# One more early table, a merged gram unit and a reordered chunk 2 in a DLRM interaction tower

## The chip, the cores and the metric

One Trainium2 chip, one core. The metric is the device time of one execution in microseconds (us), as the median of several runs. Its engines are named as the profile does: PE (TensorE, matmuls and transposes), DVE (VectorE), ACT (ScalarE), POOL (GpSimd, which issues the indirect gathers) and SP (SyncE, which issues the plain DMAs).

## What is computed

512 samples have 27 categorical features each. Every feature has a table of rows of 128 floats (1,000 to 125,000 rows). For each sample the 27 rows are looked up, all dot products of two different rows are taken, and a small dense network follows:

```python
e = jnp.stack([tbl_0[ids[:, 0]], ..., tbl_26[ids[:, 26]]], axis=1)   # 512 x 27 x 128
interactions = jnp.einsum('bfd,bgd->bfg', e, e)                      # 27 x 27 per sample
x = interactions.reshape(B, F * F)[:, TRIL_IDX]                      # 351 pairs
z = jnp.concatenate([bottom_mlp_out, x], axis=1)
h = jnp.concatenate([z, r_bottom_mlp_out], axis=1)                   # 607
h = jnp.maximum(h @ W_top1 + b_top1, 0.0)                            # 512
h = jnp.maximum(h @ W_top2 + b_top2, 0.0)                            # 256
y = h @ W_top3                                                       # 512 x 1
```

## The kernel before, in words

The samples are worked on in four chunks of 128. What a chunk needs is its transposed embeddings `ET` (128 values on the partitions, then sample and feature). They come in two ways.

Features whose table has 1,000 rows can be looked up without a gather. `plan_tables` (L49) picks `N_ONE_HOT` = 9 of the twelve such tables as early ones, which serve all four chunks, and `N_LATE` = 2 late ones, which serve chunks 2 and 3. SP loads each whole table (0.5 MB, two DMAs, L273 and L274) and the feature's ids as int16, broadcast to all partitions (L269), into a ring of `TABLE_RING` = 5 buffers. ACT casts the table to fp32r (`high`, `make_high`, L352), DVE subtracts to get the remainder (`low`, L462, four parts). The one-hot matrix `hot` of 8 blocks of 125 rows by 512 samples is made by DVE (L465, 7 or 6 blocks) and ACT (L363 and L368, 1 or 2 blocks). PE multiplies (`look_up`, L551): 8 blocks with `high` and 8 with `low`, in the order high 0 to 3, low 0 to 3, high 4 to 7, low 4 to 7, 512 columns each (256 for a late table). ACT moves the sum into `ET` (`move_lookup`, L371). `hot`, `high` and `low` are double buffered, so table n is prepared only when table n-2 is looked up. Ahead of the first table PE runs `sum(WARM_UP)` = 34 matmuls on zeros (L545).

All other features are gathered: POOL issues one indirect DMA per feature and chunk (L309), 128 rows of 512 bytes, chunk after chunk: 18 each for chunks 0 and 1, 16 each for chunks 2 and 3, 68 in all. Neighbouring features form a run of up to four; `runs` (L113) lists them, and the last run of chunk 3 is split in two. PE transposes a run into one of two PSUM banks (`transpose_run`, L523), and DVE (even runs) or ACT (odd runs) moves it to `ET` (`move_run`, L317). A run waits on PE for its rows and for the mover of the run two before it (`free_pt`, L515).

A chunk's pair products are grams (`gram_unit`, L602, L613): for 32 groups of four samples a small matmul per sample, in units of 16 groups for chunks 0 to 2 and of 8 for chunk 3 (`sizes`, L106). When a unit is done, DVE and ACT copy half of it each into `Z` (`move_gram`, L325, eight copies per engine). When all units of a chunk are copied, SP packs the rows with five small DMAs (`pack`, L244, and `pack_extra`, L250); for chunk 3 SP, ACT and POOL share them. Then come layer 1 (`dense_layer1_bottom`, L591, and three calls of `pair_tile`, L618, here called the pairs), relu on ACT (`relu_h1`, L395), layer 2 on PE (`dense_layer2`, L530) and layer 3 on DVE (`dense3`, L473, bias add, then product and sum).

Every engine has its order written out by hand, and each runs its instructions strictly in that order. On PE, chunk c's loop (L631) does the first gram unit of c, `BETWEEN[c]` runs of c+1, the pairs of c-1, the second unit of c, more runs, layer 2 of c-1, the rest of the runs. The pairs of chunk 2 stand inside chunk 3's grams (L678, `AFTER_DENSE1`, between the second and the third unit), layer 2 of chunk 2 behind them:

```python
            for k in units_of(LAST):
                if k == AFTER_DENSE1:
                    wait_packed(LAST - 1)
                    for t in range(TILES):
                        done = pair_tile(LAST - 1, t)
                    done.then_inc(dense1, 1)
                gram_unit(k)
            dense_layer2(LAST - 1)
```

The functions that the change touches, and what calls them:

## Time and profile before

| | us |
|---|---|
| median of the runs | 121.84 |
| lowest and highest of the 3 runs | 120.61, 122.99 |
| the profiled execution, its own time | 119.64 |
| its span, first to last instruction | 117.5 |

| engine | busy, us | share of the span |
|---|---|---|
| PE | 92.8 | 79% |
| DVE | 74.8 | 64% |
| ACT | 63.7 | 54% |
| POOL | 72.8 | 62% |

How to read it: the span is that of one profiled execution, and every time in a row is counted from its start. Busy time leaves out waiting; it says how much an engine had to do, not whether the end waited for it. An entry such as `[1.84 <-DMA rows<-in_tbl,ids_sb]` in a timeline says that the engine was idle for 1.84 us before the instruction and what ended that time. The matmuls of grams and layers appear as two records each in the trace; lookups, transposes and warm-ups as one. Start and length of rows overlap by a little, since matmuls and copies are pipelined; rates are therefore taken from start to start.

### The profile page before, as it was taken

The numbers are of one execution on the slowest core, as the hardware profiler recorded it, in microseconds if no ns is written. First come the engines' busy times: TensorE is split into PE (matmuls) and PEld (weight loads), VectorE is DVE, ScalarE is ACT, GpSimd is POOL, SyncE is SP. The second block draws the span as 40 slices with busy tenths as digits, with TensorE's granted clock in tenths as the row PEclk, the third lists the DMA queues.
The fourth block names the chain that finished last, engine by engine and source line by source line (L and its number), as shares of the span: only waits on it lengthen the run. The fifth ranks groups of instructions, "written<-read, shape, count | busy, mean of one in ns | idle before, by whom it ended". The sixth has DMA issues, their size and how long they took to land.

```text
span 117.5 us, 3583 instructions
## 1 busy us (share of the span) xinstructions
PE 92.8 (79%) x1464; PEld 77.8 (66%) x1464; DVE 74.8 (64%) x230; ACT 63.7 (54%) x150; POOL 72.8 (62%) x75
## 2 busy tenths in 40 slices
PE   6608999999899999794458399955899838992992
PEld 6503788878688788583357299843798718980990
DVE  5418899999999999864994062164154656793001
ACT  7525698997996985563162162361165506990010
POOL 2777777777777787777777777677677620001000
PEclk9999999999999999999999967999999999999689
DMA  3749999999999767793112212113122220000000
GB/s 39 164 132 261 252 248 237 242 244 247 230 242 234 179 165 214 290 300 92 46 45 76 62 50 67 50 50 86 49 59 59 58 58 6 0 6 21 0 0 1
DMA packets 7347, 14.28 MB, mean 121 GB/s; under 512 B 2149, under 2 KB 4485, under 8 KB 7332
## 3 DMA queue, kind: packets, MB, share of 16 engines
q1 hardware_dynamic: 5104, 9.58, 32.8%
q0 software_dynamic: 2208, 4.47, 14.5%
q8 instruction: 11, 0.18, 0.6%
q14 instruction: 4, 0.03, 0.1%
q10 hardware_dynamic: 20, 0.01, 0.1%
HBM read 13.81 MB, written 0.00 MB: 118 GB/s over the span
## 4 chain that ended last, share of the span: by engine, by line
POOL 59%; issue 18%; PE 10%; DMA 6%; DVE 3%; ACTq 1%; DVEq 0%
POOL rows L309 59%; PE pH L587 5%; DMA rows<-in_tbl,ids_sb 3%; DVE Z L342 3%; PE pT L587 2%; PE pG L613 2%; DMA ids_sb<-in_ids 2%; DMA Z<-Z 1%; PE pF L538 1%; ACTq L247 1%; PE pT L527 1%; DVE prod L484 0%; DVE ET L321 0%; DVEq L129 0%
## 5 line engine op out<-in xcount | busy, mean ns | idle before, releaser
L309 POOL DMA_INDIRECT rows<-in_tbl,ids_sb x68 | 71.6, 1054 | 21.6 <-issue 20.4
L465 DVE TENSOR_SCALAR hot<-ids_b,row_f 125x512 fp32r<-125x512 int16 (+1 forms) x75 | 31.8, 452 | 1.7 <-DMA ids_b<-in_ids_t 1.7
L342 DVE COPY Z<-pG 26x96 f32<-26x96 f32 (+1 forms) x80 | 19.5, 244 | 19.5 <-PE pG L613 18.5
L342 ACT COPY Z<-pG 26x96 f32<-26x96 f32 (+1 forms) x80 | 18.7, 234 | 16.3 <-PE pG L613 15.4
L563 PE MATMUL pG<-hot,high 125*128 125x512 f32 x72 | 22.0, 422 | 4.7 <-ACT high L352 4.2
L563 PE MATMUL pG<-hot,low 125*128 125x512 f32 x72 | 20.2, 404 | 0.0
L462 DVE TENSOR_TENSOR low<-tbl,high 125x256 fp32r<-125x256 f32 x44 | 18.2, 414 | 3.1 <-ACT high L352 3.1
L563 PEld LDWEIGHTS pG<-hot,high 125*128 125x128 f32 x72 | 13.6, 196 | 9.3 <-ACT high L352 4.5
L613 PE MATMUL pG<-ET 128*26 128x26 f32 x1024 | 13.5, 194 | 7.1 <-issue 4.6
L613 PEld LDWEIGHTS pG<-ET 128*26 128x26 f32 x1024 | 11.2, 104 | 10.1 <-issue 7.9
L563 PEld LDWEIGHTS pG<-hot,low 125*128 125x128 f32 x72 | 14.1, 196 | 3.1
L352 ACT CAST high<-tbl 125x1024 fp32r<-125x1024 f32 x11 | 11.5, 1048 | 8.2 <-DMA tbl<-in_tbl 5.9
L527 PE MATMUL pT<-ident,rows 128*128 128x128 f32 x68 | 11.4, 291 | 5.6 <-DMA rows<-in_tbl,ids_sb 1.8
L587 PE MATMUL pH<-Z,W1Z 128*128 128x128 f32 x84 | 12.2, 311 | 1.9 <-DMA Z<-Z 1.9
L527 PEld LDWEIGHTS pT<-ident,rows 128*128 128x128 f32 x68 | 8.1, 145 | 7.9 <-issue 3.0
L587 PEld LDWEIGHTS pH<-Z,W1Z 128*128 128x128 f32 x84 | 11.7, 225 | 2.3 <-DMA Z<-Z 2.2
L321 DVE COPY ET<-pT 128x256 f32<-128x256 f32 (+2 forms) x13 | 6.4, 494 | 6.7 <-PE pT L527 6.6
L321 ACT COPY ET<-pT 128x512 f32<-128x512 f32 (+3 forms) x12 | 5.8, 488 | 8.3 <-PE pT L527 8.2
L363 ACT ACTIVATE away<-ids_b,row_f 125x512 f32<-125x512 int16 x13 | 9.4, 722 | 0.1
L368 ACT ACTIVATE hot<-away 125x512 fp32r<-125x512 f32 x13 | 8.2, 633 | 0.4
L538 PE MATMUL pF<-W2S,H1T 128*128 128x256 f32 x32 | 7.7, 383 | 0.0
L247 POOL DMA_DIRECT2D Z<-Z x1 | 0.6, 555 | 11.5 <-DVE Z L342 11.5
(39 smaller groups left out, 57.6 us busy)
## 6 DMA issues: line engine op xcount, KB each, us to landing
tbl<-in_tbl SPq DMA_DIRECT2D x11, 448.0 KB
ids_b<-in_ids_t SPq DMA_DIRECT2D x9, 128.0 KB, 5.2
rows<-in_tbl,ids_sb POOLq DMA_INDIRECT x68, 5.0
W1Z<-in_w_tiles SPq DMA_DIRECT2D x1, 768.0 KB
tbl<-in_tbl SPq DMA_DIRECT2D x11, 52.0 KB
W1A_B<-in_w_ab SPq DMA_DIRECT2D x1, 512.0 KB, 3.8
W2S<-in_W_top SPq DMA_DIRECT2D x1, 512.0 KB
botT<-in_bottom_t SPq DMA_DIRECT2D x1, 256.0 KB, 4.0
```

Source lines behind the costliest of these rows:

```text
L309: pool.indirect_dma_start(out=rows[:, c % 2, slot[f], :], out_offset=None, in_=tables[f][:, :], in_offset=bass.IndirectOffsetOnAxis(ap=ids ...
L321: engine_copy(ET[:, c, :, f0:f0 + n, :].rearrange("d q f a -> d f q a"), pT[pt_order.index((c, i)) % 2][:, 0:n * P].rearrange("d (f q a) - ...
L342: last = engine_copy(to[:, :, STAGE - n:STAGE, :, s, :], of)
L352: nc.scalar.copy(high[0:TP, n % 2, :, :], tbl[0:TP, n % TABLE_RING, :, :]).then_inc(high_done, 1)
L363: nc.scalar.activation(away[0:TP, :], ids_b[0:TP, n % TABLE_RING, :], ACT.Abs, scale=-1.0, bias=row_f[0:TP, k:k + 1]).then_inc(away_done, 1)
L462: nc.vector.tensor_tensor(low[0:TP, n % 2, at, :], tbl[0:TP, n % TABLE_RING, at, :], high[0:TP, n % 2, at, :], ALU.subtract).then_inc(low_ ...
L465: nc.vector.tensor_scalar(hot[0:TP, n % 2, k, columns(n)], ids_b[0:TP, n % TABLE_RING, columns(n)], row_f[0:TP, k:k + 1], None, ALU.is_equ ...
L527: last = nc.tensor.transpose(bank[:, x * P:(x + 1) * P], rows[:, c % 2, slot[f], :], ident[:, :])
L538: last = nc.tensor.matmul(pF[:, :], H1T[:, k, :], W2S[:, k, :], start=k == 0 and c < LAST, stop=k == K1 - 1)
L563: last = nc.tensor.matmul(lookup_bank(n), part[0:TP, n % 2, k, :], hot[0:TP, n % 2, k, columns(n)], start=x == 0 and k == 0, stop=x == 3 a ...
L587: done = nc.tensor.matmul(bank[:, at * P:(at + 1) * P], weights[:, k * P:(k + 1) * P], acts, start=first and clears, stop=last, skip_group ...
L613: last = nc.tensor.matmul(pG[QUAD * s:QUAD * s + GRAM_ROWS, at:at + TOGETHER * COLS], some.rearrange("d s f -> d (s f)")[:, 0:GRAM_ROWS], ...
```

## The change

- `N_ONE_HOT` is 10: feature 14 becomes an early table, features 17 and 25 are the late ones. Gathers per chunk are 17, 17, 15 and 15, 64 in all. Chunks 2 and 3 have one run more than before (7 and 8).
- Warm-up is 72 matmuls. Table 0 is loaded and cast in two halves of four blocks (`pieces`), with a semaphore of its own for the first half.
- SP no longer waits for the first ids before it asks for table 1, nor for the last table or `W1A_B` before it asks for the weights.
- DVE makes all one-hot blocks of a table first and then the four `low` parts; `look_up` runs high 0 to 7, then low 0 to 7. ACT moves the lookup of table n-1 ahead of the one-hot blocks of table n+1.
- Grams of chunks 0 to 2 are one unit of 32 groups each. Chunk 3 keeps four units of 8, with nothing between them.
- `prepare` and `look_up` of the late tables, layer 1 and 2 of each chunk, and relu and layer 3 get new places. Layer 1, relu, layer 2 and layer 3 of chunk 2 all stand inside chunk 2's loop, ahead of the last runs of chunk 3. The wait for the weights moves from the first loop to `dense_layer2`.
- `packed` is one semaphore per chunk.

The diff, cut to its core (names of the new lines are those of the changed kernel):

```diff
-N_ONE_HOT = 9
+N_ONE_HOT = 10
...
-WARM_UP = (20, 14)
+WARM_UP = 72
...
-    sizes = [[16, 16]] * LAST + [[8, 8, 8, 8]]
+    sizes = [[32]] * LAST + [[8, 8, 8, 8]]
...
+        def pieces(n):
+
+            return 1 + (n == 0)
...
                 elif n >= IN_FLIGHT:
                     sp.wait_ge(tbl_in[n - IN_FLIGHT], 32)
-                elif n:
-                    sp.wait_ge(ids_b_in[n - 1], 16)
...
-            sp.wait_ge(tbl_in[N_ALL - 1], 32)
             sp.dma_start(W1A_B[:, :, :], w1_ab).then_inc(w1ab_in, 16)
...
-            sp.wait_ge(w1ab_in, 16)
...
                 if n + 1 < N_ONE_HOT:
                     make_high(n + 1)
-                    one_hot_blocks(n + 1)
                 if n:
                     move_lookup(n - 1)
+                if n + 1 < N_ONE_HOT:
+                    one_hot_blocks(n + 1)
...
                 for k in range(TABLE_K - act_blocks[n]):
-                    part = k - 1
-                    if 0 <= part < LOW_PARTS:
...
                     nc.vector.tensor_scalar(hot[0:TP, n % 2, k, columns(n)], ids_b[0:TP, n % TABLE_RING, columns(n)],
                                             row_f[0:TP, k:k + 1], None, ALU.is_equal).then_inc(hot_done, 1)
+                for at in (slice(k, k + step) for k in range(0, TABLE_K, step)):
+                    dve.wait_ge(high_done, n + 1 + (n > 0 or at.stop > TABLE_K // 2))
+                    nc.vector.tensor_tensor(low[0:TP, n % 2, at, :], tbl[0:TP, n % TABLE_RING, at, :],
+                                            high[0:TP, n % 2, at, :], ALU.subtract).then_inc(low_done, 1)
...
+                runs_of(c + 1, 2, 4)
                 if c:
                     dense3(c - 1)
-                runs_of(c + 1, RUNS[c + 1] - LATE_RUNS[c + 1], RUNS[c + 1])
+                if c + 1 == LAST:
+                    dense3(c)
+                runs_of(c + 1, 4, RUNS[c + 1])
...
+                for k in units_of(c):
+                    gram_unit(k)
+                next_run()
+                next_run()
                 if c == 0:
                     look_up(N_ONE_HOT)
+                    next_run()
+                    look_up(N_ONE_HOT + 1)
+                    next_run()
+                    dense_layer1_bottom(c)
                 else:
+                    dense_layer1_pairs(c - 1)
+                    next_run()
+                    dense_layer2(c - 1)
+                if c + 1 < LAST:
+                    while len(waiting):
+                        next_run()
+                    if c:
+                        dense_layer1_bottom(c)
+                else:
+                    dense_layer1_bottom(c)
+                    dense_layer1_pairs(c)
+                    next_run()
+                    dense_layer2(c)
+                    while len(waiting):
+                        next_run()
...
             for k in units_of(LAST):
-                if k == AFTER_DENSE1:
-                    wait_packed(LAST - 1)
-                    for t in range(TILES):
-                        done = pair_tile(LAST - 1, t)
-                    done.then_inc(dense1, 1)
                 gram_unit(k)
-            dense_layer2(LAST - 1)
```

Where instructions stand now. First PE at the start of the program (`warm` is the warm-up operand, `hot`, `high` and `low` those of the lookup, x the count of equal instructions in a row). Before:

```order
L545 MATMUL pF<-warm 128x128 x34
L563 MATMUL pG<-hot,high 128x512 x4
L563 MATMUL pG<-hot,low 128x512 x4
L563 MATMUL pG<-hot,high 128x512 x4
L563 MATMUL pG<-hot,low 128x512 x4
```

And in the changed kernel:

```order
L541 MATMUL pF<-warm 128x128 x72
L557 MATMUL pG<-hot,high 128x512 x8
L557 MATMUL pG<-hot,low 128x512 x8
L557 MATMUL pG<-hot,high 128x512 x8
L557 MATMUL pG<-hot,low 128x512 x8
L522 MATMUL pT<-ident,rows 128x128 x2
```

The warm-up is more than twice as long, and a table's lookup is one group of eight with `high` and one with `low`.

Second, PE from chunk 2's grams to chunk 3's (`pG<-ET` are grams, `pT<-ident,rows` transposes of gathered rows, `pH<-botT,W1AB` the bottom part of layer 1, `pH<-Z,W1Z` the pairs, `pF<-W2S,H1T` layer 2). Before:

```order
L613 MATMUL pG<-ET 26x26 x64
L587 MATMUL pH<-botT,W1AB 128x128 x4
L587 MATMUL pH<-Z,W1Z 128x128 x12
L613 MATMUL pG<-ET 26x26 x64
L527 MATMUL pT<-ident,rows 128x128 x6
L538 MATMUL pF<-W2S,H1T 128x256 x4
L587 MATMUL pH<-botT,W1AB 128x128 x4
L527 MATMUL pT<-ident,rows 128x128 x10
L613 MATMUL pG<-ET 26x26 x64
L587 MATMUL pH<-Z,W1Z 128x128 x12
L613 MATMUL pG<-ET 26x26 x64
L538 MATMUL pF<-W2S,H1T 128x256 x4
```

And in the changed kernel:

```order
L607 MATMUL pG<-ET 26x26 x128
L522 MATMUL pT<-ident,rows 128x128 x6
L581 MATMUL pH<-Z,W1Z 128x128 x12
L522 MATMUL pT<-ident,rows 128x128 x2
L534 MATMUL pF<-W2S,H1T 128x256 x4
L581 MATMUL pH<-botT,W1AB 128x128 x4
L581 MATMUL pH<-Z,W1Z 128x128 x12
L522 MATMUL pT<-ident,rows 128x128
L534 MATMUL pF<-W2S,H1T 128x256 x4
L522 MATMUL pT<-ident,rows 128x128 x6
L607 MATMUL pG<-ET 26x26 x128
```

The pairs of chunk 1 moved behind the first two runs of chunk 3, and the pairs and layer 2 of chunk 2 moved from inside and behind chunk 3's grams to before its last transposes.

Third, DVE at the same place (`Z<-pG` are copies of grams, `ET<-pT` moves of transposed runs, `H<-pF,b_sb` and `prod,y<-H,W3S` the two instructions of layer 3). Before:

```order
L342 COPY Z<-pG 26x2x3x8x2 x3
L342 COPY Z<-pG 26x10x8x2
L321 COPY ET<-pT 128x2x64x2 x2
L321 COPY ET<-pT 128x4x64x2
L481 TENSOR_TENSOR H<-pF,b_sb 128x256
L484 SCALAR_TENSOR_TENSOR prod,y<-H,W3S 128x256
L321 COPY ET<-pT 128x64x2
L342 COPY Z<-pG 26x2x3x4x2 x3
```

And in the changed kernel:

```order
L343 COPY Z<-pG 26x160x2
L322 COPY ET<-pT 128x2x64x2 x2
L477 TENSOR_TENSOR H<-pF,b_sb 128x256
L480 SCALAR_TENSOR_TENSOR prod,y<-H,W3S 128x256
L477 TENSOR_TENSOR H<-pF,b_sb 128x256
L480 SCALAR_TENSOR_TENSOR prod,y<-H,W3S 128x256
L322 COPY ET<-pT 128x64x2
L322 COPY ET<-pT 128x2x64x2
L343 COPY Z<-pG 26x2x3x4x2 x3
```

Layer 3 of chunk 2, which stood behind all copies of chunk 3, now stands ahead of the moves of chunk 3's runs 4 and 6.

## Rows read from the trace of the kernel before

**Rows 1.** The page, 40 equal slices: busy tenths of PE, granted clock.

```profile
PE   6608999999899999794458399955899838992992
...
PEclk9999999999999999999999967999999999999689
```

**Rows 2.** The page: chain that ended last, by engine; the gathers' group.

```profile
POOL 59%; issue 18%; PE 10%; DMA 6%; DVE 3%; ACTq 1%; DVEq 0%
...
L309 POOL DMA_INDIRECT rows<-in_tbl,ids_sb x68 | 71.6, 1054 | 21.6 <-issue 20.4
```

**Rows 3.** Windows of L309: stretch, its length, busy (count), PEclk, DMA share, GB/s.

```profile
9.35:48.88 39.53, 31.61 (x26) 1.00 0.96 237
48.88:93.92 45.04, 34.06 (x37) 0.96 0.27 77
```

**Rows 4.** Timeline of POOL: start, length, what, idle before.

```profile
40.72 1.65 POOL L309 DMA_INDIRECT rows<-in_tbl,ids_sb  x1 [0.30 <-issue]
```

**Rows 5.** Timeline of all engines, from 92 us to the end.

```profile
92.08 3.06 SPq L247 DMA_DIRECT2D Z<-Z  x4
...
93.92 0.94 POOL L309 DMA_INDIRECT rows<-in_tbl,ids_sb  x1 [0.31 <-issue]
...
95.11 0.41 DVE L481 TENSOR_TENSOR H<-pF,b_sb 128x256 f32<-128x256 f32 x1
...
96.30 0.61 PE L527 MATMUL pT<-ident,rows 128*128 128x128 f32 x3 [1.84 <-DMA rows<-in_tbl,ids_sb]
...
97.34 1.32 PE L613 MATMUL pG<-ET 128*26 128x26 f32 x128 [0.43 <-DVE ET L321]
...
98.12 3.56 DVE L342 COPY Z<-pG 26x48 f32<-26x48 f32 x16 [0.88 <-PE pG L613]
...
102.26 3.56 DVE L342 COPY Z<-pG 26x48 f32<-26x48 f32 x16 [0.57 <-PE pG L613]
...
108.94 2.48 PE L587 MATMUL pH<-Z,W1Z 128*128 128x128 f32 x12 [1.85 <-DMA Z<-Z]
...
111.46 0.38 ACT L403 ACTIVATE H1T<-pH 128x256 f32<-128x256 f32 x1 [5.77 <-PE pH L587]
...
113.32 1.89 PE L538 MATMUL pF<-W2S,H1T 128*128 128x256 f32 x8
```

**Rows 6.** Timeline of PE, warm-up, table 0, and the first grams.

```profile
1.14 3.81 PE L545 MATMUL pF<-warm 128*128 128x128 f16 x34 [1.14 <-DVE warm L443]
9.16 3.12 PE L563 MATMUL pG<-hot,high 125*128 125x512 f32 x4 [4.21 <-ACT high L352]
12.07 1.90 PE L563 MATMUL pG<-hot,low 125*128 125x512 f32 x4
...
15.66 1.07 PE L563 MATMUL pG<-hot,high 125*128 125x512 f32 x4
...
48.84 1.81 PE L613 MATMUL pG<-ET 128*26 128x26 f32 x128 [0.73 <-issue]
```

**Rows 7.** Timelines of SP, DVE and ACT, 5 to 14 us.

```profile
6.25 0.43 SPq L273 DMA_DIRECT2D tbl<-in_tbl  x1
...
5.94 0.49 DVE L465 TENSOR_SCALAR hot<-ids_b,row_f 125x512 fp32r<-125x512 int16 x1 [1.66 <-DMA ids_b<-in_ids_t]
...
13.68 0.42 DVE L462 TENSOR_TENSOR low<-tbl,high 125x256 fp32r<-125x256 f32 x1 [0.34 <-ACT high L352]
...
8.06 1.04 ACT L352 CAST high<-tbl 125x1024 fp32r<-125x1024 f32 x1 [3.65 <-DMA tbl<-in_tbl]
...
12.61 1.04 ACT L352 CAST high<-tbl 125x1024 fp32r<-125x1024 f32 x1 [2.21 <-DMA tbl<-in_tbl]
```

**Rows 8.** Timelines of PE (two calls of the pairs) and DVE (copies of a unit of 16).

```profile
69.48 3.98 PE L587 MATMUL pH<-Z,W1Z 128*128 128x128 f32 x24
...
84.89 2.84 PE L587 MATMUL pH<-Z,W1Z 128*128 128x128 f32 x24
...
89.82 2.23 DVE L342 COPY Z<-pG 26x96 f32<-26x96 f32 x8 [2.98 <-PE pG L613]
```

More of the change, by code:

```diff
@@ L550, in look_up @@
                     pe.wait_ge(lookup_moved, n)
-                half = TABLE_K // 2
-                first, second = range(half), range(half, TABLE_K)
-                for x, (part, blocks) in enumerate(((high, first), (low, first), (high, second), (low, second))):
-                    if x == 0:
-                        pe.wait_ge(high_done, n + 1)
-                    for k in blocks:
+                for part in (high, low):
+                    for k in range(TABLE_K):
+                        if part is high and k % (TABLE_K // 2) == 0:
+                            pe.wait_ge(high_done, n + 1 + (n > 0 or k > 0))
                         if part is high and k < TABLE_K - act_blocks[n]:
@@ L564, in look_up @@
                                                 hot[0:TP, n % 2, k, columns(n)],
-                                                start=x == 0 and k == 0, stop=x == 3 and k == TABLE_K - 1)
+                                                start=part is high and k == 0, stop=part is low and k == TABLE_K - 1)
                 last.then_inc(looked_up, 1)
```

114 lines of the change are left out of this document (41 added, 73 removed).

## The prediction

> **What bounds the kernel now.** I read the page first, by slices, then the chain of waits, then the timelines of the stretches that the chain names. The slices show three stages: up to about 50 us (slice 17; a slice is 2.94 us) PE is at nine tenths; then it is half idle; its clock falls twice, in slices 23 and 24 and in 37 and 38 [rows 1]. The chain that ended last says what limits the middle: 59% of the span is POOL at the gathers of L309, and 18% "issue", mostly the pause between two of them, so POOL issues 68 gathers without one wait on another engine [rows 2]. The timeline of POOL gives the pace. 26 gathers issued from 9.35 to 48.88 us are 39.53 / 26 = 1.520 us apart, the 36 that start from 48.88 on are 45.04 / 36 = 1.251 us apart (the view counts 37, the one that starts at its end with them), with the DMA engines 96% busy at 237 GB/s in the first stretch and 27% in the second [rows 3]; the last starts at 93.92 [rows 5]. PE's wait for those rows ends at 96.30, 2.4 us later; grams of chunk 3 start at 97.34; 20.16 us from there to the end of the span (117.5) are a serial tail [rows 5]. So the time is: gathers until 93.92, 3.42 us to the grams, then the tail.
>
> The one-hot stage (9 to 48 us) isn't on that chain, but PE, DVE and ACT are all full in it, so a tenth table could put it there. The profiled execution took 119.64 us outside for a span of 117.5; the median of the runs shown is 121.84. I work in the span of the profile and add the difference to the median. Under about 2% (2.4 us) a change can hardly be told from none here.
>
> **The gathers.** Ten early tables instead of nine: features that are still gathered fall from 18, 18, 16, 16 per chunk to 17, 17, 15, 15, so 64 instead of 68. Four fewer at 1.251 us is 5.0 us off POOL's queue [rows 3]. Against it stands the slower pace during the one-hot stage: 26 x (1.520 - 1.251) = 7.0 us were lost there, with nine tables' work on DVE beside it. At 7.0 / 9 the tenth costs 0.8 us. Bounds: nothing (then the last gather starts at 88.9), and all 26 gathers at the worst row, 1.65 + 0.30 = 1.95 us apart, 11 us more [rows 4]; I take 0.8, as the total of DVE's work grows by a ninth and only its order changes. The last gather then starts at 93.92 - 5.0 + 0.8 = 89.7.
>
> The Trainium skill has a rule that speaks against this change: in "SBUF — State Buffer", section "SBUF: two separate sides", it says that while VectorE is in a two-port performance mode GpSimd is locked out and "cannot write the descriptors" of its DMAs. Taken whole, it would make VectorE's one-hot instructions, now six or seven in a row, a price on each gather beside them. By it the sum would be that of rival B below; by the row's 0.8 us it is the one here. The trace agrees in part (1.52 against 1.25 us), but the pace also goes with a full DMA, and no run here parts the two.
>
> **The one-hot stage.** One table is 16 matmuls of 512 columns; four take about 0.91 us from start to start, so 3.65 us, and with transposes and waits before, 8 tables from 15.66 to the end of the stage (48.84 less the 0.7 us of the last move) took 32.4 us, 4.05 each [rows 6]. The tenth table costs PE 4.05 us. What pays for it is the start. In before, PE warms until 4.95, then waits 4.21 us; its first four matmuls take 3.12 us, as each waits for a one-hot of DVE, which makes one at 5.94 and then stands behind the high part, started by ACT at 8.06; the next four take 1.90 us instead of 1.07, that is the clock's lower level, 1.2 GHz instead of 2.4; table 0 ends at 15.66 [rows 6, 7]. In after DVE makes all seven of table 0's one-hots from 5.94 on, before anything waits on it; the table arrives in two halves, and 72 warm-ups (34 x 0.112 = 3.8 us, then 38 at 0.056 to 0.112) keep PE busy until 7.1 to 9.2. Table 0 is then 3.65 us, ending near 12. Table 1 was cast from 12.61 on because it was asked for only at 6.25 [rows 7]; SP doesn't wait for the ids any more and asks at about 4. Its 0.63 MB (0.50 of table, 0.13 of ids) at 237 GB/s [rows 3] behind table 0 (8.1) is an estimate of 10.7 to 11, no later than 12.6 at worst. PE starts table 1 at about 12.0 instead of 15.66, and 9 x 4.05 = 36.5 brings the end to 48.5 instead of 48.1: the tenth table is free to within half a microsecond (from -1 to +2). DVE agrees: its lows of table 1 start at about 12.1 instead of 13.68 [rows 7], its one-hots of that table are already made, and from there it had no idle time in before. The order high x 8, low x 8 costs nothing: the lows are needed 1.8 us later than before. The gram unit of 32 in chunks 0 to 2 costs PE nothing (same 128 matmuls); on DVE and ACT 8 copies of double size replace 16. Eight copies of a unit of 8 take half of 3.56 us, 1.78 [rows 5]; of a unit of 16, 2.23 [rows 8]; 0.45 us for doubling 56 elements on the mean gives +0.9 for doubling 112, so 3.1 us instead of 4.46. Bounds: 2.23 and 4.46. They start one unit later, and the packing of chunk 2 rests on them, below.
>
> Would the rest of the stage hold up the middle? Chunk 1's grams follow about 13 us behind chunk 0's start (two late tables, their moves, the last runs): 62 instead of about 65. From there PE has 9 us of work (grams, runs, layer 1 and 2 of chunk 0), to 71. Chunk 2's last row is gather 49, issued at 89.7 - 15 x 1.251 = 70.9, landed near 73.9. So there are 3 us of cover: the early stage may be 3 us late and cost nothing.
>
> **Chunk 2 and the chain to the last grams.** This is where the order hurts. The rows for run 1 of chunk 3 end with gather 55, issued at 89.7 - 9 x 1.251 = 78.4. With a landing of 2.4 us [rows 5] to half as much again, 3.6 (an estimate; I take 3.0) PE may transpose at 81.4. Behind those transposes there now stand, in order on PE, both chunks' layers. Prices: layer-1 pairs 2.84 us for 24 records [rows 8], bottom a third of that (8 records, 0.95), layer 2 1.89 less the 0.15 in which its last record only ends, the relu's first half 0.38 [rows 5]. So: transposes to 81.9; pairs(1) to 84.75; relu 85.15; layer 2 (1) 86.9; bottom(2) 87.8; pairs(2) 90.7 (its packing: grams of chunk 2 from 75.2, 2.7 us, copies 3.1, five issues by SP 3.8, as four take 3.06 [rows 5], and under 2 to land, as copies end at 105.82 and PE starts at 108.94 in the tail with two issues between, 86.6, so hidden by 1.2 us); relu and hand-off 91.15; layer 2 (2) 93.1 with its latency. DVE has layer 3 of chunk 2 in front of the move of run 4 (0.41 us and about as much for its second half, 0.9 in all [rows 5]): 94.0; move 94.3. Run 6 shares run 4's bank, so it is transposed only now; from transposes to grams took 97.34 - 96.30 = 1.04 us [rows 5]: 95.3, and 0.3 us for some ten hand-offs: grams of chunk 3 at 95.6. The rows of gather 64 are there at 92.1 to 93.3. So 5.0 us taken off POOL move the grams by 97.34 - 95.6 = 1.7 us only; the rest goes into layer 1 and 2 of chunk 2, which now stand ahead of the last grams.
>
> **The tail.** Before: 0.78 us to the first copy, 16 copies, a wait of 0.57 for the third unit (PE had pairs(2) in between), 16 copies, end 105.82: 8.5 us. After: the four units' grams are in one piece, so 0.78 + 32 x 0.2225 = 7.9 us. From there on the chain is the same, 117.5 - 105.82 = 11.7 us [rows 5]. 95.6 + 7.9 + 11.7 = 115.2. The clock: pairs(3) ran 4.38 us from 108.94 to 113.32 instead of 2.84, and two slices show 6 and 8 tenths after PE had done 0.2 of a slice [rows 1, 5]. PE is now idle for some 7 us before it, so all of it may be at the lower level: up to 2 x 2.84 - 4.38 = 1.3 us more. It may also find the same phase. I take 0.4. Forecast span 115.6, 1.9 us less, on the median 121.84 - 1.9 = 119.9.
>
> **The rivals.**
> (A) The clock falls on the new chain. PE has only two transposes between chunk 2's grams (77.9) and 81.4. A gap like this stood before the pairs of chunk 0: 24 records took 3.98 us instead of 2.84 [rows 8], slices 6 and 7 [rows 1]. Price 1.1 to 1.9 us on the chain and up to 1.3 in the tail: 115.2 + 1.5 + 1.3 = 118.0 (median 122.3), just slower than before. Against: other thin stretches (slices 18, 19, 21) left it at 9. It decides when both falls come, over 2.3 us.
> (B) DVE's one-hots in a row hold POOL harder. The one gather of 1.65 us lay in such a stretch [rows 4]. If gathers beside them (60% of the stage) are issued every 1.95 us and others every 1.52, the mean is 1.78, 26 x 0.26 = 6.8 us more than my pace, everything behind POOL: 115.6 + 6.8 - about 1 that the lesser pace saves elsewhere, 121 to 122 (median 126). It beats the gain from 2 us of added issue time on. Against: DVE's total is the same, and another gather beside such a stretch is not slow.
> (C) The gain comes out whole: rows land in 2.4 us, the added 0.8 doesn't show, and pairs(3) finds the higher level: 115.2 - 0.8 - 0.6 - 1.5 = 112.3 (median 116.7).
> (D) The change doesn't do what it says: PE's own pauses ("issue" in the grams, hand-offs) fill the chain: 117.5 as before.
>
> **How the numbers follow.** Forecast 0.40 (114.6 to 116.5 in span, medians 118.9 to 120.8), A 0.20, B 0.08, C 0.18, D 0.14. Faster by over 2% means a median under 119.4: all of C and 0.16 of the forecast, 0.34, say 0.35. Slower by over 2%, over 124.3: B and 0.02 of A, 0.10. The rest 0.55. The range takes in C but for its far end and A: 117.5 to 122.6.
>
> **What would show it.** Right: 64 gathers, the last starting at 89 to 90.5; table 1's matmuls at about 12 and chunk 0's grams at 48 to 50; chunk 3's run 1 waiting for its rows until 81 to 82; pairs(1), pairs(2) and layer 2 back to back behind it; PE's last wait before the grams for DVE, not for rows; grams at 95 to 96.5; 32 copies without a gap; idle PE before pairs(3) some 7 us. Wrong: grams right behind the last rows (then the chain was shorter than I say), gathers of 1.5 us and more in the one-hot stage (B), PEclk at 5 around 82 to 86 (A), or chunk 2's grams later than 77, with PE never waiting for rows in chunk 2.

## The result and the profile after

The changed kernel took 132.75 us (median of four, 131.88 to 134.15); the kernel before took 121.22 us beside it (120.29 to 122.99). The ratio is 1.0955, 95% interval [1.0818, 1.1092]. Forecast were 119.9 us and a range of 117.5 to 122.6. A ratio here and below is formed from the executions within about 1.5% of the fastest of their kernel, a median from all of them, so a ratio can differ a little from the quotient of the medians. The profiled execution took 132.68 us for a span of 130.9, 13.4 us more than before.

Three places part those 13.4 us: the last gather starts at 103.09 instead of 93.92 (+9.2, forecast -4.2); from there to the grams of chunk 3 it is 6.50 instead of 3.42 us (+3.1); from the grams to the end 21.3 instead of 20.2 (+1.1).

The page of the kernel after (busy tenths of PE and POOL, granted clock; the gathers' group and the chain by engine), to be held against [rows 1, 2]:

```profile
PE   6978899999459499975759758848398875536792
...
POOL 2879888999978888987777877777778600001000
PEclk9999999999977999999999999999999999755579
...
POOL 51%; issue 16%; PE 15%; DVE 6%; DMA 6%; SPq 2%; ACTq 1%; ACT 0%; DVEq 0%
...
L310 POOL DMA_INDIRECT rows<-in_tbl,ids_sb x64 | 81.9, 1280 | 20.5 <-issue 18.6
```

There are 64 gathers, four fewer, but they keep POOL busy 81.9 us instead of 71.6: 1280 ns for one instead of 1054. PE has holes in slices 10, 11 and 13 (counted from 0), where in [rows 1] it was full until slice 17. The windows say in which stretch the gathers became slow:

```profile
9.00:55.60 46.60, 40.20 (x22) 0.96 0.86 221
55.60:103.09 47.49, 35.91 (x39) 1.00 0.22 58
```

From 55.6 us on it is 47.49 / 38 = 1.250 us from gather to gather, as in [rows 3] (39 are counted with the one that starts at the end). Before that, 22 gathers take 46.6 us: 2.12 us each, against 1.52. So the pace behind the one-hot stage is as before; the loss sits in that stage, beside a DMA that is less busy (0.86) than it was before (0.96). The timeline of POOL and DVE in that stage shows it in single instructions:

```profile
14.30 1.83 POOL L310 DMA_INDIRECT rows<-in_tbl,ids_sb  x1 [0.30 <-issue]
15.13 2.85 DVE L457 TENSOR_SCALAR hot<-ids_b,row_f 125x512 fp32r<-125x512 int16 x7
...
21.96 1.42 DVE L461 TENSOR_TENSOR low<-tbl,high 125x256 fp32r<-125x256 f32 x4
22.46 3.81 POOL L310 DMA_INDIRECT rows<-in_tbl,ids_sb  x1 [0.30 <-issue]
23.30 2.85 DVE L457 TENSOR_SCALAR hot<-ids_b,row_f 125x512 fp32r<-125x512 int16 x7
26.08 1.41 DVE L461 TENSOR_TENSOR low<-tbl,high 125x256 fp32r<-125x256 f32 x4
26.58 3.74 POOL L310 DMA_INDIRECT rows<-in_tbl,ids_sb  x1 [0.30 <-issue]
...
27.76 2.44 DVE L457 TENSOR_SCALAR hot<-ids_b,row_f 125x512 fp32r<-125x512 int16 x6
30.13 1.41 DVE L461 TENSOR_TENSOR low<-tbl,high 125x256 fp32r<-125x256 f32 x4
30.63 3.81 POOL L310 DMA_INDIRECT rows<-in_tbl,ids_sb  x1 [0.30 <-issue]
31.47 2.85 DVE L457 TENSOR_SCALAR hot<-ids_b,row_f 125x512 fp32r<-125x512 int16 x7
...
51.77 3.93 POOL L310 DMA_INDIRECT rows<-in_tbl,ids_sb  x1 [0.30 <-issue]
...
53.40 2.18 DVE L457 TENSOR_SCALAR hot<-ids_b,row_f 125x256 fp32r<-125x256 int16 x8
```

A gather that is under way when DVE begins its row of seven one-hots (23.30) ends at 26.27, 0.12 us behind the row (26.15). The next begins during the low parts, meets the next row and ends with it (30.32 and 30.20). Three times in a row the same, and again at 51.77 beside the eight short one-hots of a late table. It is not so with every row: of the eleven gathers under way when a row of six or more began, these four ended with the row; the seven others ended inside it, 0.2 to 1.0 us after its start, and took 0.94 to 2.62 us, as the one of 14.30, which ends at 16.13 while its row lasts until 17.98. The four alone are some 10.6 us over gathers of 1.16 us; the longer ones among the others make up the rest of the 13.4 us by which the last gather missed the forecast.

From the rows of chunk 3's run 1 to the last grams, PE of the kernel after, to be held against [rows 5] and the second order above:

```profile
94.42 0.66 PE L522 MATMUL pT<-ident,rows 128*128 128x128 f32 x4 [0.43 <-DMA rows<-in_tbl,ids_sb]
94.91 2.84 PE L581 MATMUL pH<-Z,W1Z 128*128 128x128 f32 x24
...
98.32 1.97 PE L534 MATMUL pF<-W2S,H1T 128*128 128x256 f32 x8 [0.27 <-ACT H1T L407]
100.12 1.05 PE L581 MATMUL pH<-botT,W1AB 128*128 128x128 f32 x8
101.91 2.95 PE L581 MATMUL pH<-Z,W1Z 128*128 128x128 f32 x24 [0.74 <-DMA Z<-Z]
...
105.42 1.97 PE L534 MATMUL pF<-W2S,H1T 128*128 128x256 f32 x8 [0.46 <-ACT H1T L407]
...
108.67 0.52 PE L522 MATMUL pT<-ident,rows 128*128 128x128 f32 x3 [0.96 <-DVE ET L322]
109.59 1.34 PE L607 MATMUL pG<-ET 128*26 128x26 f32 x128 [0.41 <-DVE ET L322]
112.84 1.70 PE L607 MATMUL pG<-ET 128*26 128x26 f32 x127 [1.92 <-DVE Z L343]
116.64 0.24 PE L607 MATMUL pG<-ET 128*26 128x26 f32 x1 [2.10 <-issue]
```

The two chunks' layers stand between the transposes at 94.42 and the grams at 109.59: 15.2 us in a row, of which only the last two waits are DVE's. The last line shows a third thing, that no term of the forecast had: one gram matmul waits 2.10 us for "issue", that is for nothing that the profile shows on another engine.

### The profile page after: what moved, and what is told of

It is laid out like the page before. It is cut to its first block, busy times and chain, and to the rows that moved or that the text cites. A ratio compares the mean times of both kernels' runs of the same rounds, so it can differ in the third digit from the quotient of the medians.

```text
span 130.9 us, 3675 instructions
## 1 busy us (share of the span) xinstructions
PE 99.7 (76%) x1514; PEld 83.6 (64%) x1514; DVE 75.2 (57%) x217; ACT 64.0 (49%) x134; POOL 83.0 (63%) x71
## 4 chain that ended last, share of the span: by engine, by line
POOL 51%; issue 16%; PE 15%; DVE 6%; DMA 6%; SPq 2%; ACTq 1%; ACT 0%; DVEq 0%
POOL rows L310 51%; PE pH L581 5%; DVE Z L343 5%; PE pG L607 5%; PE pF L534 3%; DMA Z<-Z 3%; SPq L249 2%; DMA rows<-in_tbl,ids_sb 2%; PE pT L581 2%; DMA ids_sb<-in_ids 1%; ACTq L249 1%; PE pT L522 1%; DVE prod L480 1%; DVE ET L322 0%; DVE H L477 0%
## 5 line engine op out<-in xcount | busy, mean ns | idle before, releaser
L310 POOL DMA_INDIRECT rows<-in_tbl,ids_sb x64 | 81.9, 1280 | 20.5 <-issue 18.6
L343 DVE COPY Z<-pG 26x48 f32<-26x48 f32 (+3 forms) x56 | 15.9, 284 | 17.8 <-PE pG L607 17.1
L343 ACT COPY Z<-pG 26x48 f32<-26x48 f32 (+3 forms) x56 | 15.0, 268 | 22.5 <-PE pG L607 21.8
L355 ACT CAST high<-tbl 125x1024 fp32r<-125x1024 f32 (+1 forms) x13 | 12.8, 983 | 13.8 <-PE pG L557 7.9
L557 PEld LDWEIGHTS pG<-hot,high 125*128 125x128 f32 x80 | 15.4, 201 | 6.4 <-ACT high L355 1.8
L322 DVE COPY ET<-pT 128x256 f32<-128x256 f32 (+3 forms) x14 | 6.3, 450 | 10.0 <-PE pT L522 9.9
L366 ACT ACTIVATE away<-ids_b,row_f 125x512 f32<-125x512 int16 x15 | 10.9, 724 | 0.2
L249 POOL DMA_DIRECT2D Z<-Z x1 | 0.6, 555 | 15.2 <-DVE Z L343 15.2
L371 ACT ACTIVATE hot<-away 125x512 fp32r<-125x512 f32 x15 | 9.5, 632 | 0.5
L322 ACT COPY ET<-pT 128x512 f32<-128x512 f32 (+2 forms) x13 | 5.7, 437 | 7.1 <-PE pT L522 7.0
L407 ACT ACTIVATE H1T<-pH 128x256 f32<-128x256 f32 x7 | 2.4, 385 | 13.0 <-PE pH L581 13.0
```

The lines of the kernel that those rows point to most:

```text
L310: pool.indirect_dma_start(out=rows[:, c % 2, slot[f], :], out_offset=None, in_=tables[f][:, :], in_offset=bass.IndirectOffsetOnAxis(ap=ids ...
L322: engine_copy(ET[:, c, :, f0:f0 + n, :].rearrange("d q f a -> d f q a"), pT[pt_order.index((c, i)) % 2][:, 0:n * P].rearrange("d (f q a) - ...
L343: last = engine_copy(to[:, :, STAGE - n:STAGE, :, s, :], of)
L355: nc.scalar.copy(high[0:TP, n % 2, ks, :], tbl[0:TP, n % TABLE_RING, ks, :]).then_inc(high_done, 1)
L366: nc.scalar.activation(away[0:TP, :], ids_b[0:TP, n % TABLE_RING, :], ACT.Abs, scale=-1.0, bias=row_f[0:TP, k:k + 1]).then_inc(away_done, 1)
L371: nc.scalar.activation(hot[0:TP, n % 2, k, :], away[0:TP, :], ACT.Relu, scale=-1.0, bias=1.0).then_inc(hot_act_done, 1)
```

## The experiments

Times of different runs are compared by their ratio to the kernel before on the same chip. On three chips the kernel before itself took 159 to 162 us. In the traces taken there, the kernels with ten tables have table transfers that stood still for 12 to 20 us; in the two with nine tables the transfers flow, and PE takes 39 and 38 us instead of 1.8 for the first gram unit, with pauses of 0.4 to 2.6 us between single matmuls. Of the runs there only the lengths of gathers and waits are used, not the times.

The theories. L (lock): a row of one-hots on DVE holds a gather that POOL has under way, up to the row's end; rows of six or seven cost the time, not DVE's total. F (fuller queue): the gathers are slow because SP asks for tables and weights earlier. C (chain): the layers of chunk 2 ahead of the last grams cost what they take, since PE and not the rows ends last there.

**1. The changed kernel with one-hots and low parts in turn.** Everything else stays, the earlier requests of SP too, so L and F part here.

```diff
                 for k in range(TABLE_K - act_blocks[n]):
+                    part = k - 1
+                    if 0 <= part < LOW_PARTS:
+                        ...
+                        nc.vector.tensor_tensor(low[...], tbl[...], high[...], ALU.subtract)
                     nc.vector.tensor_scalar(hot[...], ids_b[...], row_f[...], None, ALU.is_equal)
-                for at in (slice(k, k + step) for k in range(0, TABLE_K, step)):
-                    ...
```

> The changed kernel with DVE's order of before inside a table (one-hot, low, one-hot, low ... instead of seven one-hots and then four lows); all else stays. Theory L (one-hots in a row hold POOL's gather until the row ends): no gather over 2 us, the last of 64 starts at 89 to 91 us instead of 103.1, chunk 3's grams at 96 to 98, span 117 to 119 us, 12 to 14 us under the changed kernel. Theory F (the fuller DMA queue, asked for earlier and by one table more, slows the gathers): gathers of 3.8 us stay, the last starts after 100, span over 127. Theory C (the moved layers of chunk 2 and the tail cost most of it): span not under 127 either, though the gathers are faster.

> The changed kernel with DVE's order of before inside a table, run again, because the kernel before took 162 us beside it in the first go. Where the kernel before takes about 121 us: theory L (one-hots in a row hold POOL's gather until the row ends) expects the last gather at 89 to 91 us instead of 103.1, chunk 3's grams at 96 to 98, span 117 to 119 us. Theory F (fuller DMA queue) and theory C (moved layers and tail): span over 127.

> The changed kernel with DVE's order of before inside a table, third go, wanted beside a kernel before of about 121 us. Theory L (one-hots in a row hold POOL's gather until the row ends): last gather at 89 to 91 us instead of 103, chunk 3's grams at 96 to 98, span 117 to 120 us, ratio 0.97 to 1.00. Theory F (fuller DMA queue) and theory C (moved layers and tail): span over 127, ratio over 1.05.

The first two runs fell on chips of 160 us and more (170.86 against 162.03; 168.59 against 159.96): as times they say nothing of L. Their longest gathers were 2.05 and 1.56 us. The third was usable: 127.21 us (125.99 to 128.75) against 121.35, ratio 1.057 [1.041, 1.073]. DVE and POOL of this run:

```profile
26.79 0.48 DVE L464 TENSOR_SCALAR hot<-ids_b,row_f 125x512 fp32r<-125x512 int16 x1
27.19 0.42 DVE L461 TENSOR_TENSOR low<-tbl,high 125x256 fp32r<-125x256 f32 x1
27.27 1.16 POOL L310 DMA_INDIRECT rows<-in_tbl,ids_sb  x1 [0.30 <-issue]
...
28.65 0.42 DVE L461 TENSOR_TENSOR low<-tbl,high 125x256 fp32r<-125x256 f32 x1
28.73 1.65 POOL L310 DMA_INDIRECT rows<-in_tbl,ids_sb  x1 [0.30 <-issue]
28.99 1.27 DVE L464 TENSOR_SCALAR hot<-ids_b,row_f 125x512 fp32r<-125x512 int16 x3
```

A gather beside hot, low, hot takes 1.16 us; beside three one-hots in a row (28.99 to 30.26) it takes 1.65 us and ends with them, at 30.38. No gather of this run is longer. The last starts at 89.92; the forecast had 89.7. The order of DVE's instructions is what made the gathers slow: L stands, F falls. The runs show what the order does, and not by which shared part of the chip DVE holds POOL. But the grams of chunk 3 still start only at 105.25, 15.3 us behind the last gather: the 13 us that came back on POOL brought 4 on the end. I had expected 96 to 98 for these grams and a ratio of 0.97 to 1.00.

**2. The kernel before with one-hots in a row.** The converse: one edit in the kernel before, of DVE's order alone.

```diff
                 for k in range(TABLE_K - act_blocks[n]):
-                    part = k - 1
-                    if 0 <= part < LOW_PARTS:
-                        ...
                     nc.vector.tensor_scalar(hot[...], ids_b[...], row_f[...], None, ALU.is_equal)
+                for at in (slice(k, k + step) for k in range(0, TABLE_K, step)):
+                    ...
```

> The kernel before, and only DVE's order inside a table changed to that of the changed kernel (all one-hots, then four lows). Theory L: ten tables lost about 21 us of POOL's time in the changed kernel against 1.251 us per gather, so nine lose 19 instead of 7: the last gather starts at 105 to 107 instead of 93.9, span 129 to 131. Theory F and C: nothing in the DMA queues or in chunk 2 is changed, span 117 to 119.

> The kernel before with only DVE's order inside a table changed to one-hots in a row, run again for the same reason. Theory L: the last gather starts at 105 to 107 instead of 93.9, span 129 to 131. Theories F and C: 117 to 119.

> The kernel before with one edit: VectorE makes all one-hots of a table in a row and the four low parts behind them. Lock theory (a row of one-hots holds the gather that POOL has begun until the row ends): gathers of 2.5 to 4 us stand in the one-hot stage, the last gather starts 4 to 8 us later than 93.9, so at 98 to 102, and since the rows bound this kernel the end moves as far: span 122 to 126, ratio 1.04 to 1.07. If the lock needs the changed kernel's other edits (ten tables, the fuller queue): longest gather below 2.5 us, last gather within 1.5 us of 93.9, ratio within 1.02.

On chips of 160 us it took 165.07 (before 162.03) and 166.08 (before 159.96), with gathers of 4.61 and 3.51 us. On a usable one 127.56 us (125.29 to 131.06) against 123.08, ratio 1.026 [1.016, 1.036], less than I expected. Its profile (131.06 us, the longest execution of the six) has the row again:

```profile
40.78 3.52 POOL L309 DMA_INDIRECT rows<-in_tbl,ids_sb  x1 [0.31 <-issue]
41.31 2.87 DVE L458 TENSOR_SCALAR hot<-ids_b,row_f 125x512 fp32r<-125x512 int16 x7
44.08 1.44 DVE L462 TENSOR_TENSOR low<-tbl,high 125x256 fp32r<-125x256 f32 x4
44.60 3.14 POOL L309 DMA_INDIRECT rows<-in_tbl,ids_sb  x1 [0.30 <-issue]
45.42 2.20 DVE L458 TENSOR_SCALAR hot<-ids_b,row_f 125x256 fp32r<-125x256 int16 x8
```

40.78 + 3.52 = 44.30, the row's end is 44.18. The last gather starts at 103.66, 9.7 us later than before. So the row alone makes the kernel slower, with nine tables and the old requests. Here two of the gathers under way ended with the row of six or more, in the kernel after four; how many are held so long varies from run to run, and what decides it isn't shown.

**3. The changed kernel once more, as it is.**

> The changed kernel as it is, to have its trace and its ratio on the chips on which the kernel before took 160 to 162 us in the last two goes. All theories: if the chip is like those of the result, 131 to 134 us against 121. If it is like those of the last two goes, theory L expects gathers of 2 to 4 us where DVE makes one-hots in a row, and a ratio above the 1.075 of the interleaved kernel there; theory F and C the same ratio as that one, 1.06 to 1.09.

132.87 us (129.24 to 134.97) against 121.72; gathers of 3.81, 3.54 and 2.62 us and the last one at 101.40. The loss repeats, though only two of the gathers under way when a row began (3.81 and 3.54 us) ended with it; the rest of POOL's loss is in gathers of 1.7 to 2.6 us. The medians give 1.092; the shortest executions, 129.24 and 120.19 us, 1.075.

**4. The layers of chunk 2 late again**, in a kernel with one-hots in turn and in one with one-hots in a row. On PE (DVE and ACT follow):

```diff
                     dense_layer1_bottom(c)
-                    dense_layer1_pairs(c)
-                    next_run()
-                    dense_layer2(c)
...
             for k in units_of(LAST):
+                if k == UNITS_BY[LAST] - 2:
+                    dense_layer1_pairs(LAST - 1)
                 gram_unit(k)
+            dense_layer2(LAST - 1)
```

In turn:

> As the run before, and the pairs, relu, layer 2 and layer 3 of chunk 2 where the kernel before has them (inside and behind chunk 3's grams). If the chain of layers ahead of the last grams is what keeps the gain of fewer gathers away: chunk 3's grams start about 3.4 us after the last gather's start, as in before, at 93 to 94, and the tail is 20.2 us as before: span 113 to 115, 3 to 4 us less than the run before it. If that chain costs nothing: the same span as that run, 117 to 119.

> The same with the pairs, relu, layer 2 and layer 3 of chunk 2 where the kernel before has them, second go. If the chain of layers ahead of the last grams keeps the gain away: chunk 3's grams about 3.4 us after the last gather's start, at 93 to 94, span 113 to 115, ratio 0.95 to 0.97, 3 to 5 us under the run before it. If that chain costs nothing: the same span as that run.

In a row:

> The changed kernel with the layers of chunk 2 placed as before (pairs between the second and third gram unit of chunk 3, layer 2 behind the fourth, ReLU and layer 3 of chunk 2 as late), one-hots still in a row. With both theories (the lock sets the last gather, the early layers add to what follows it): last gather still at 101 to 103, grams of chunk 3 start 3.5 to 5 us behind it and not 6.5, tail 20 to 21, span 125 to 128, time 127 to 130 against 132.8. If the early layers were hidden under the wait for rows: the grams of chunk 3 start 6.5 us behind as before and the tail is longer by the moved layers, time 132 to 134. If they are worth the 7 us that they were with interleaved one-hots: 125 to 126.

The first went to a chip of 160 us (163.25 against 162.03). Usable: with one-hots in turn 120.07 us (119.15 to 122.44) against 121.35, ratio 1.000 [0.993, 1.007]; with one-hots in a row 128.50 (126.98 to 128.91) against 123.08, 1.047 [1.027, 1.067], last gather at 101.91 and grams of chunk 3 at 105.19, 3.3 us behind it. Four ratios make a table:

```
                     one-hots in a row   one-hots in turn
layers early              1.096               1.057
layers late               1.047               1.000
```

The row costs 3.9 and 4.7 points, the early layers 4.9 and 5.7: 5 to 6 us and 6 to 7 us of 121. Each ratio is known to 1 to 2 points, so the two add up as well as can be told (with the 1.075 above in the first corner the early layers would be 3 points there). L and C are both shown, and together they are the whole loss.

**5. Why nothing is gained without them.** In the last corner of the table the last gather starts at 89.72, 4.2 us before [rows 5], and the time is that of the kernel before. Page (chain) and timeline of PE of that kernel:

```profile
PE 68%; DVE 13%; issue 8%; DMA 5%; ACT 2%; SPq 1%; ACTq 1%; DVEq 0%
...
15.04 2.00 PE L559 MATMUL pG<-hot,high 125*128 125x512 f32 x8
...
52.18 3.47 PE L609 MATMUL pG<-ET 128*26 128x26 f32 x217 [0.73 <-issue]
...
86.15 0.66 PE L609 MATMUL pG<-ET 128*26 128x26 f32 x35 [2.23 <-issue]
86.74 1.54 PE L524 MATMUL pT<-ident,rows 128*128 128x128 f32 x6
88.08 3.50 PE L583 MATMUL pH<-Z,W1Z 128*128 128x128 f32 x24
...
97.22 1.32 PE L609 MATMUL pG<-ET 128*26 128x26 f32 x128 [0.40 <-ACT ET L322]
```

The chain that ended last is PE's at 68%, and POOL, 59% in [rows 2], isn't on it. Table 1 starts at 15.04; from there to the end of the stage (51.45) it is 36.4 / 9 = 4.05 us a table, to the digit the forecast's. What was wrong is the start: forecast 12.0. (The two other usable runs with one-hots in turn for all tables start table 1 at 14.42 and 17.00.) PE never waits for rows any more, and the last grams come 7.5 us behind the last gather. I had expected them at 93 to 94 us and a ratio of 0.95 to 0.97. I looked for what could make PE shorter. In that kernel the unit of 32, split in two of 16:

```diff
-    sizes = [[32]] * LAST + [[8, 8, 8, 8]]
+    sizes = [[16, 16]] * LAST + [[8, 8, 8, 8]]
```

> The changed kernel with one-hots interleaved, the layers of chunk 2 late, and two gram units of 16 again in chunks 0 to 2 (in a row, one behind the other). Theory that the unit of 32 costs time, since VectorE and ScalarE copy a bank of 32 grams (3.2 us) only behind the last of its 256 matmuls and the transposes' copies stand behind: the grams of chunks 1 and 2 start 1 to 1.5 us earlier each, last grams at 94.5 to 95.5, time 117.5 to 118.5. Rival: TensorE's pauses of 1 to 2 us inside the gram matmuls cost it, whatever the unit: pauses of the same sum (6 us), time 119.5 to 120.5.

120.67 us (119.09 to 122.76) against 121.50, ratio 1.002 [0.993, 1.012]; "issue" in the grams is 6.9 us in sum against 6.4 with units of 32. The rival holds: the unit costs nothing, the pauses stay, as long as the two units stand behind one another. Then, again in the kernel of the last corner, the first table's one-hots in a row, the others in turn:

```diff
                     part = k - 1
-                    if 0 <= part < LOW_PARTS:
+                    if n and 0 <= part < LOW_PARTS:
...
+                for at in (slice(k, k + step) for k in range(0, TABLE_K if n == 0 else 0, step)):
```

> The changed kernel with one-hots and low parts interleaved for all tables but the first, whose seven one-hots stay in a row (they begin before POOL has gathers under way for long), and the layers of chunk 2 placed late. Theory that TensorE sets the time from the one-hot stage on once the lock is gone: table 1 starts at about 13.9 as in the changed kernel rather than 15.0, the grams of chunk 0 at 51, of chunk 3 at 96, last gather at 90 to 92, time 119 against 120.1 with all tables interleaved. Rival: one row of seven already holds a gather by 2 to 3 us, last gather at 92 to 93, and nothing is gained: 120 to 121.

120.75 us (118.45 to 122.05) against 123.08 (121.23 to 127.6). Table 1's first matmul came at 12.51 instead of 15.04, but the next ones then waited one by one for DVE's one-hots, and the grams of chunk 0 began at 52.17, as without it. The longest gather took 2.05 us. By the medians that is 0.98 of the kernel before beside it, where the last corner has 0.99 (120.07 against 121.35); with four executions and no interval, nothing is shown to be gained.

**6. Terms of the change alone, in the kernel before.** The early start (warm-up of 72, table 0 in halves, SP's wait for the first ids gone), the tenth table, and both:

```diff
-WARM_UP = (20, 14)
+WARM_UP = (40, 32)
...
-                elif n:
-                    sp.wait_ge(ids_b_in[n - 1], 16)
```

```diff
-N_ONE_HOT = 9
+N_ONE_HOT = 10
```

> The kernel before with ten early tables and nothing else changed. The step of the prediction on the gathers: the last of 64 starts at 89 to 90.5. The one-hot stage ends about 4 us later (52 instead of 48), as nothing starts earlier; if 3 us of cover are there, the span falls by 2 to 4 us to 114 to 116; if the stage is on the path, it stays at 117 or more.

> The kernel before with the early start alone (warm-up of 72, first table in two halves, SyncE's waits behind the first ids taken away), nine tables. Its rows bound it, so the start of TensorE is worth nothing if POOL stays as it is: last gather 93.5 to 95, time within 1 us of before. The forecast's term (table 1 starts 3.66 us earlier) would show as table 1 at 12 and not at 15.66, by the profile of the interleaved version it starts at 15.0 (0.6 us earlier), since VectorE makes hots and lows in turn.

> The kernel before with ten tables by one-hots and nothing else. Forecast's terms: last gather at 89.7, one-hot stage 4.05 us longer on TensorE (grams of chunk 0 at 52.9 and not 48.84). Theory that TensorE is then the bound: last grams at 97 to 98, span and time within 1 us of before (-0.5 to +1). Rival: before's order of two units hides it, last grams at 94 to 95, time 3 us less.

> The kernel before with ten tables and the early start, its own order of one-hots, gram units and layers. If the early start gives TensorE 0.6 us at table 1 and it is the bound: 0.5 to 1 us less than ten tables alone, time 119 to 121 with before at 121.3. If the early start gives the 3.66 us of the forecast: 3 us less than ten tables alone. This is the version that could beat both kernels.

> The kernel before with ten tables and the early start, once more, with more rounds. TensorE as the bound from the one-hot stage on: grams of chunk 0 at 52 to 53.2, last gather at 89.5 to 90.5 where no single gather is long, last grams at 96 to 99, ratio 0.985 to 1.005. If the 4.2 us of the gathers came through: last grams at 93 to 95, ratio 0.965 to 0.98.

The tenth table alone was first at 163.80 us on a chip of 162.03. On a usable chip, before 121.50 (119.0 to 125.03): early start alone 125.03 (121.99 to 125.5), tenth table alone 126.75 (124.41 to 127.04), both 121.80 (117.61 to 124.66). The last gathers started at 93.86, 89.62 and 98.33 (there one gather took 11.56 us, which no other run shows). Each has four executions and no interval; the shortest ones are 121.99, 124.41 and 117.61 against 119.0. Both once more met a chip of 159 us (160.63 against 159.43). So the first two missed my expectation by 3.5 and 5 us, and neither by its rows; for both together I had expected 119 to 121 us. Timeline of PE with the tenth table alone:

```profile
56.37 0.36 PE L563 MATMUL pF<-hot,high 125*128 125x256 f32 x1
61.36 1.01 PE L563 MATMUL pF<-hot,high 125*128 125x256 f32 x3 [4.62 <-issue]
62.17 1.05 PE L563 MATMUL pF<-hot,low 125*128 125x256 f32 x4
...
70.98 2.04 PE L587 MATMUL pH<-botT,W1AB 128*128 128x128 f32 x8 [3.03 <-DVE W1AB L501]
```

PE stands still for 4.62 us, then four matmuls take 1.05 us (0.64 in the kernel before, at the higher clock, 2.4 GHz; here the granted clock is 0.50, the level of 1.2), then it waits 3.03 us for DVE's sum of the bottom weights. With the early start alone a pause of 5.04 us stands at 49.3 to 54.3. What ends such a pause is in the DMA's own table, below. The wait for the sum I tried to take away, by putting the sum ahead of the last half table's one-hots:

```diff
-                    prepare(N_ONE_HOT + 1)
                     dve.wait_ge(w1ab_in, 16)
                     nc.vector.tensor_tensor(W1AB[:, :], W1A_B[:, 0, :], W1A_B[:, 1, :], ALU.add)
+                    prepare(N_ONE_HOT + 1)
```

> The same with VectorE's sum of the bottom weights ahead of the one-hots of the last half table and not behind them. If TensorE is the bound: its wait of 3 us before the bottom layer of chunk 0 shrinks to under 1 us, of which its next product takes back up to 1 us (that table's one-hots come 0.7 us later), and the end comes 1 to 2.5 us earlier than in e2_again. If the rows bound it, the wait shrinks and the time is the same within 0.5 us.

160.30 us on the chip of 159.43, where the stalled tables cover this place: it tells nothing. No version here is shown to beat the kernel before.

## Why the prediction was wrong, step by step

- "Ten early tables instead of nine": right. 64 gathers, and 1.25 us each where DVE isn't making one-hots.
- "I take 0.8, as the total of DVE's work grows by a ninth and only its order changes": **the step that failed first.** The order was the cost. 22 gathers in 46.6 us instead of 26 in 39.5 put the last one at 103.09 instead of 89.7. With one-hots in turn the step is right to 0.2 us in two runs (89.92, 89.72) and 2.0 us late in a third (91.74). My upper bound, every gather at 1.95 us, was the row beside three one-hots; I read a bound for rows of seven from it. The line of DVE beside it, in the kernel before:

```profile
40.98 1.27 DVE L465 TENSOR_SCALAR hot<-ids_b,row_f 125x512 fp32r<-125x512 int16 x3
```

These three end at 42.25 and the gather of 40.72 at 42.37, the same 0.12 us behind. That a longer row could hold a gather longer was to be read from it.

- Rival B named the mechanism at 0.08 and 126 us. "Another gather beside such a stretch is not slow" was my argument against it; it is true of some gathers also in the kernel after (0.94 us at 48.97, with a row from 49.67), and says nothing of those that are held. The Trainium skill's rule in "SBUF — State Buffer", section "SBUF: two separate sides", calls the shared port pair "an exclusive lock, not a bandwidth split", held "for the whole instruction". The trace agrees in part: four gathers of 3.74 to 3.93 us were held across six to eight instructions, not one, and seven others got through inside a row.
- "Table 1 at about 12.0": 13.87 in the kernel after and 15.04 with one-hots in turn, against 15.66 before. The term of 3.66 us was worth 1.8 and 0.6. DVE's first one-hot, which I had at 5.94 as before, came at 7.29, behind a wait of 3.02 us for the ids (at 6.65 with the tenth table alone, where SP's waits are as before). "9 x 4.05" was right (4.05), so the stage ends at 51.45 instead of 48.5 (15.04 + 36.4), even where nothing holds the rows.
- "There are 3 us of cover": **the second step that failed.** Cover was counted against POOL, from a stage that ended 3.5 us too early, and without the pauses in the grams. With one-hots in turn and late layers the grams start at 52.18, 66.21, 80.31 and 97.22, where I had 49.2 (the stage's 48.5 and the last move), 62, 75.2 and 95.6.
- The chain from gather 55 to the last grams: right in kind, 15.2 us where I had 14.2 (rows landed in 2.57 us, but pairs(2) waited 0.74 for its packing, which I had hidden by 1.2). Its meaning was wrong: I let it eat 3.3 us of POOL's gain, but taking it out of the way gave back 6 to 7 us of time, because PE comes to it late anyway.
- The unit of 32: 3.16 and 3.18 us for eight copies, forecast 3.1; no effect on the time.
- The tail: 7.9 us forecast for the copies; they ended at 118.68, 9.1 us behind the grams, since PE's waits of 1.92 us (for DVE's copies) and 2.10 us ("issue") stand in it. The lower clock of rival A came in the tail (slices 35 to 37 at 5), but not on the chain before it (slices at 9). One reading of mine against that rival was off: slice 21 is not thin (8 tenths), 20 and 22 are (5 and 3).

## What to carry over

Where DVE works beside POOL's gathers as here, look at the order of its instructions and not at their sum. One-hots in turn with low parts leave a gather at 1.16 us or so (0.94 where DVE makes none, with an idler DMA too); the same seven in a row held some gathers until the row's end, at up to 2.8 us more each, and others for up to 1.5 us. Work that "rows hide" is hidden only as long as PE isn't the bound itself; before a step is moved ahead, take away the bound on paper and see which engine ends last. And a gain of fewer gathers is to be counted only up to the next engine: here the last gather came 4.2 us earlier and the time stayed.

## What the runs showed of the hardware

**A row of one-hots can hold a gather until the row ends.** Above: 3.81, 3.74, 3.81 and 3.93 us for gathers of 1.2 us, each ending 0.12 us behind the row of one-hots beside it. It doesn't always: seven of eleven in the kernel after, and ten of twelve in its second run, ended inside the row. Being under way when the row begins isn't what decides; a gather begun inside a row (20.48, 1.68 us) ends with it too.

**Pauses in the grams go with instruction loads.** The page of the kernel after lists a queue of instructions, and the DMA view of short windows (0.25 us from 60.50 and from 114.25) has one packet of it each:

```profile
q8 instruction: 12, 0.20, 0.6%
...
q8 instruction: 1, 0.02, 23.6%
...
q8 instruction: 1, 0.02, 23.3%
```

12 packets for PE's 3028 matmuls and weight loads are 252 a packet, and 0.20 MB / 12 is 17 KB. The pause in chunk 0's grams of the kernel after, and that of its tail, stand so to the packets:

```profile
57.54 3.48 PE L607 MATMUL pG<-ET 128*26 128x26 f32 x217 [0.73 <-issue]
63.05 0.53 PE L607 MATMUL pG<-ET 128*26 128x26 f32 x39 [2.04 <-issue]
```

The packet starts at 60.5 to 60.75, the pause ends at 63.05; that of 114.25 to 114.5 ends at 116.64; with late layers the packets of the windows from 83.25 and 54.0 go with pauses that end at 86.15 and 56.63; the long pause of 4.62 us has its packet in the window from 58.75 and ends at 61.36, the one of 5.04 in that from 51.75 and ends at 54.31. From the packet's start to the pause's end it is 2.2 to 2.9 us, and it is so for all 32 pauses of over 0.75 us in the grams of the twelve traces that are not from the chips of 160 us. 256 gram matmuls with their weight loads are two packets' worth and run in 3.7 us, and my reading is that the loads don't keep up there; in the two long pauses the packet itself began 2.3 and 2.6 us after PE had stopped, while the weights' transfers filled the DMA engines (queue 1 had 82% of them from 54 to 57 us in the run with the tenth table alone). That PE waits for the packet is read from this distance, no run removed one; that the weights delay it is argued from two. Not every pause is of this kind: the 0.73 us ahead of chunk 0's first gram stands in every kernel without a packet at that distance, as do three short ones of the kernel before (0.30, 0.41 and 0.41), and so do those of the chips of 160 us, where no packet comes between 49.93 and 92.17 us in a unit of grams that lasts from 49.04 to 88.4 (first run of experiment 2). In the Trainium skill's "Runtime: NRT & Kernel Launch", section "Instruction fetch mechanics", crossing to the next 16 KiB block is "mostly hidden". The trace agrees on the block's size and not on the price: the pauses that go with packets sum to 2.8 us in the kernel before and 7.1 in the kernel after, and one alone reaches 5.0. Without the 0.73 us at the start, all pauses for "issue" in the grams sum to 3.9 us in the kernel before and 2.8, 6.4, 1.4 and 1.6 in the four variants with its order (grams in pieces of 128 matmuls among other work; 5.0 of the 6.4 is the one long pause), and to 7.1, 5.7, 11.0, 5.6, 6.2, 5.4 and 3.5 where 256 stand together.

**Open.** Why both terms together were 3 to 5 us faster than each alone, with so few executions each, and whether they beat the kernel before; what decides whether a row of one-hots holds a gather to its end; what makes the tables stand still, or PE pause in the grams, on some chips.
